# Spreading a second layer norm over the last pairs of a local attention and the first feed-forward

## What is computed

```
x = x + local_attention(ln_c(x))          # norm over channels, 7x7 windows, relative bias
t = to_tokens(x)
h = ln_t(t)                               # the second norm: (t - mean) / sqrt(var + 1e-5), over 64 channels
for step in 33 steps:
    op = argmax(h[0, 0, :19])             # the op decides which weights, and whether
    if attn_mask[step, op]: h = softmax(q k^T / 8) v wo      # an attention
    if ffn_mask[step, op]:  h = relu(h w1 + b1) w2 + b2      # and / or a feed-forward is run
out = t + h
```

## Time and profile before

| what | us |
|---|---|
| median of 3 runs | 248.5 (248.47 to 250.22) |
| the profiled execution, its own time | 249.26 |
| its span in the profile | 247.0 |
| PE busy in the span | 230.8 (93%) |
| DVE busy | 161.4 (65%) |
| ACT busy | 151.1 (61%) |

### The profile page before, as it was taken

One profiled execution on the slowest core, in us unless ns is written; L12 is line 12 of the kernel. 1 busy time (PEld: TensorE's weight loads), 2 busy tenths in 40 slices (PEclk: granted clock), 3 DMA queues, 4 the chain that ended last, 5 costly groups with the idle time before them and its releaser, 6 DMA issues.

```text
span 247.0 us, 5393 instructions
## 1 busy us (share of the span) xinstructions
PE 230.8 (93%) x1999; PEld 155.2 (63%) x2000; DVE 161.4 (65%) x300; ACT 151.1 (61%) x291; POOL 25.5 (10%) x37
## 2 busy tenths in 40 slices
PE   7679989999999998999899999999999999998991
PEld 3236658766777755533375787788888888886330
DVE  1535645676776644764596999897778778762642
ACT  2174462446456685464459988879887876682641
POOL 9600032212122100160000000000000000000000
PEclk9889999999999999999999999999999999999998
DMA  6500000000000001000100000000000000000006
GB/s 157 126 1 3 3 0 3 5 0 0 3 0 3 0 0 36 1 0 13 33 0 0 3 0 4 1 3 0 3 0 3 0 3 0 3 0 4 0 22 149
DMA packets 3151, 3.60 MB, mean 15 GB/s; under 512 B 1077, under 2 KB 2229, under 8 KB 3126
## 3 DMA queue, kind: packets, MB, share of 16 engines
q1 hardware_dynamic: 2486, 2.59, 4.4%
q10 hardware_dynamic: 544, 0.66, 1.0%
q0 software_dynamic: 96, 0.00, 0.0%
HBM read 2.21 MB, written 1.05 MB: 13 GB/s over the span
## 4 chain that ended last, share of the span: by engine, by line
PE 77%; DVE 6%; ACT 6%; issue 4%; DMA 2%; ACTq 2%; DVEq 1%
PE ps L649 12%; PE ps L635 11%; PE ps L614 11%; PE ps L702 6%; PE ps L716 6%; PE ps L478 5%; PE ps L466 4%; PE ps L441 4%; PE ps L332 3%; PE ps L445 3%; DMA rel_tab<-in_bias_tables 2%; PE ps L401 2%; DVE sq L1012 2%; ACT prob L813 2%; PE ps L455 1%
## 5 line engine op out<-in xcount | busy, mean ns | idle before, releaser
L935 ACT COPY arena<-ps 128x1024 f32<-128x1024 f32 x32 | 32.3, 1010 | 15.8 <-PE ps L635 15.6
L1155 DVE TENSOR_REDUCE negmax<-ps 128x1 f32<-128x1024 f32 x32 | 38.4, 1218 | 1.3 <-PE ps L614 1.1
L614 PE MATMUL ps<-h_st,g_st 128*128 128x512 f32 x128 | 38.6, 423 | 0.7 <-ACT late L883 0.4
L883 ACT ACTIVATE late<-ps,negmax 128x1024 f32<-128x1024 f32 x32 | 35.8, 1119 | 5.1 <-DVE negmax L1155 4.5
L635 PE MATMUL ps<-eye,late 128*128 128x128 f32 x256 | 33.5, 274 | 0.6 <-DVE late L1165 0.2
L635 PEld LDWEIGHTS ps<-eye,late 128*128 128x128 f32 x256 | 29.1, 141 | 6.9 <-DVE late L1165 2.7
L813 ACT ACTIVATE prob<-ps,negmax 128x308 f32<-128x308 f32 x32 | 16.3, 513 | 27.7 <-DVE negmax L1056 27.7
L649 PE MATMUL ps<-arena,late 128*64 128x128 f32 x512 | 31.5, 276 | 1.1 <-ACT arena L935 1.1
L649 PEld LDWEIGHTS ps<-arena,late 128*64 128x64 f32 x512 | 27.6, 137 | 3.8 <-issue 2.2
L614 PEld LDWEIGHTS ps<-h_st,g_st 128*128 128x128 f32 x128 | 21.7, 188 | 8.8 <-issue 3.2
L1165 DVE TENSOR_SCALAR late<-late,rinv 128x1024 f32<-128x1024 f32 x32 | 24.1, 754 | 1.1
(11 more groups left out here) (120 smaller groups left out, 318.9 us busy)
## 6 DMA issues: line engine op xcount, KB each, us to landing
out<-osum SPq DMA_DIRECT2D x8, 128.0 KB, 2.3
x<-in_x SPq DMA_DIRECT2D x2, 256.0 KB, 5.0
x<-in_x ACTq DMA_DIRECT2D x2, 256.0 KB, 6.0
onehot<-in_key_onehot SPq DMA_DIRECT2D x2, 133.0 KB, 2.8
w1d<-in_ffn_w SPq DMA_DIRECT2D x4, 64.0 KB, 2.4
w2p<-in_ffn_pack SPq DMA_DIRECT2D x2, 65.5 KB, 2.6
spread_w<-in_spread_mat SPq DMA_DIRECT2D x4, 32.0 KB, 5.5
mean_w<-in_mean_mat SPq DMA_DIRECT2D x1, 96.0 KB, 2.3
```

What stands on the lines that cost most here:

```text
L614: mm = nc.tensor.matmul(ps[:, 2 * h + c, :], g_st[:, b2, h, q0:q0 + P], h_st[:, b2, h, part, c * 512:c * 512 + 512], start=(part == 0), st ...
L883: nc.scalar.activation(pr[:, n % 2, :], ps[:, 2 * (n % 2):2 * (n % 2) + 2, :], ACT.Exp, bias=negmax[:, 0, n % 2:n % 2 + 1], accum_out=rows ...
L935: nc.scalar.copy(prt[:, n // 8 % 2, n % 2, :, q0:q0 + P], ps[:, bank:bank + 2, :].rearrange("p b (c q) -> p (b c) q", c=4)).then_inc(S["s_ ...
L1155: nc.vector.tensor_reduce(negmax[:, 0, n % 2:n % 2 + 1], ps[:, 2 * (n % 2):2 * (n % 2) + 2, :], mybir.AxisListType.XY, ALU.max, negate=Tru ...
```

## The change

The norm's chunks 0, 1 and 2 are taken into the pairs: pairs 8, 10 and 12 have `centre` (bank 7) ahead of the scores, and `mix` of that pair waits until ACT has squared and copied it; pairs 9, 11 and 13 have `variance` (bank 7), which ACT copies out with epsilon added (`copy_variance`), and `mix` waits for that copy. DVE takes the reciprocal of each in pairs 10, 12 and 14 (`turn_variance`), and one ACT instruction takes the root of all three (`root_three`) behind pair 14. `spread` and `scale` of chunks 0 to 2 stand around `mix(15)`. Chunk 3 goes into the first feed-forward if that stands alone (`first=True`), else ahead of the loop (`finish_norm`). The decision moves into pair 7, and `load_next` into pairs 9 (ACT, DVE) and 10 (PE). `keep_busy` in the norm is gone. In the first feed-forward the next `load_next` of ACT and DVE stands ahead of the last store.

```diff
 # PE, pairs 1 to 13
-                if p < 7:
-                    pe.wait_ge(S["mixed"], p)
+                pe.wait_ge(S["mixed"], p)
+                if p == 7:
+                    turn_row(7, x2f)
+                if p in (8, 10, 12):
+                    centre(p // 2 - 4, 7)
+                if p in (9, 11, 13):
+                    variance(1, (p - 9) // 2)
...
+                if p == 7:
+                    pe.wait_ge(S["decided"], 1)
+                if p == 10:
+                    load_next()
+                if p in (8, 10, 12):
+                    pe.wait_ge(S["centre_copied"], p // 2 + 1)
+                if p in (9, 11, 13):
+                    pe.wait_ge(S["var_copied"], (p - 7) // 2)
                 mix(p)
...
             turn_probs(14)
-            turn_row(1, x2f)
             turn_values(15)
-            centre(0)
             mix(14)
             turn_probs(15)
...
+            spread(1, 0)
+            spread(1, 1)
+            mix(15)
             spread(1, 2)
...
+                if first:
+                    pe.wait_ge(S["h_ready"], 2)
                 up(0, 0)
+                if first:
+                    centre_last()
                 up(0, 1)
+                if first:
+                    pe.wait_ge(S["h_ready"], 3)
+                    variance(1, 3)
+                    up(1, 0)
+                    down(0, (0,))
+                    spread(1, 3)
+                    down(0, (1,))
                 pe.wait_ge(S["h_ready"], chunks + 4)
-                up(1, 0)
+                if not first:
+                    up(1, 0)
                 up(1, 1)
-                down(0)
+                if not first:
+                    down(0)
 # ACT
+            def copy_variance(j):
+                act.wait_ge(S["var_ready"], 4 + j + 1)
+                nc.scalar.activation(sq[:, j * 512:j * 512 + P], ps[:, 7, 0:P], ACT.Identity,
+                                     bias=eps_c[:, 1:2]).then_inc(S["var_copied"], 1)
+            def root_three():
+                act.wait_ge(S["var_turned"], 3)
+                inv = sq[:, 0:3 * 512].rearrange("p (j c) -> p j c", j=3)[:, :, 0:P]
+                nc.scalar.activation(inv, inv, ACT.Sqrt).then_inc(S["rooted"], 1)
...
+                if p in (8, 10, 12):
+                    square(1, p // 2 - 4)
+                if p in (9, 11, 13):
+                    copy_variance((p - 9) // 2)
+                if p == 9:
+                    load_next()
                 exps(p + 2)
             copy_turned(14)
             load_table(ACT.Sqrt)
+            root_three()
             copy_turned(15)
...
                 for t in range(4):
                     relu(t, 0)
+                    if first and t == 0:
+                        square(1, 3)
                     relu(t, 1)
+                    if first and t == 0:
+                        root(1, 3)
                     if t > 0:
                         store(t - 1)
+                    if first and t == 1:
+                        load_table(ACT.Exp)
+                if first:
+                    load_next(1)
                 store(3)
 # DVE, pairs 1 to 13
                 copy_values(p + 1)
...
+                if p == 7:
+                    decide(0, 7)
                 maxima(p + 2)
                 add_mixed(p)
+                if p == 9:
+                    load_next()
+                if p in (10, 12):
+                    turn_variance(p // 2 - 5)
```

More of the change, by code:

```diff
@@ L215, in run_event, with run @@
                 load_next()
-            def run(attention, feed_forward):
+            def run(attention, feed_forward, finish_norm=None, first=None, loads_itself=False):
                 eng.reg_alu(alone, am, 1, op=ALU.logical_shift_left)
@@ L482, in mix @@
                 mm.then_inc(S["pv_done"], 1)
+            load_next, run, sections = routing(pe)
             pe.wait_ge(S["k_loaded"], 32)
@@ L691, in attention, with feed_forward @@
                 mix(15)
-            def feed_forward(a, f, ev, row):
+            def feed_forward(a, f, ev, row, first=False):
                 chunks = pe.snap(4 * pe.snap(a + f))
@@ L706, in up, with down @@
                     mm.then_inc(S["hid_ready"], 1)
[L708 to L712, removed]
+                def down(t, parts=(0, 1)):
+                    set0, bank = 4 * (t % 2), t // 2
+                    for i in parts:
+                        c = i ^ bank
                         pe.wait_ge(S["relu_act"], 8 * f + 2 * t + i + 1)
@@ L737, in feed_forward @@
                 down(3)
-            run(attention, feed_forward)
+            run(attention, feed_forward, finish_norm, partial(feed_forward, first=True))
         @block.scalar
@@ L826, in copy_turned @@
                 ins.then_inc(S["pt_copied"], 1)
+            load_next, run, sections = routing(act)
             copy_queries(0)
@@ L961, in feed_forward @@
                     relu(t, 0)
+                    if first and t == 0:
+                        square(1, 3)
                     relu(t, 1)
+                    if first and t == 0:
+                        root(1, 3)
                     if t > 0:
                         store(t - 1)
+                    if first and t == 1:
+                        load_table(ACT.Exp)
+                if first:
+                    load_next(1)
                 store(3)
-            run(attention, feed_forward)
+            run(attention, feed_forward, finish_norm, partial(feed_forward, first=True), True)
         @block.vector
@@ L1084, in add_mixed, with decide @@
                                         ALU.add).then_inc(S["mixed"], 1)
+            def decide(n, bank, ev=None):
+                dve.wait_ge(S["row_turned"], n + 1)
+                if ev is not None:
+                    dve.wait_ge(S["info_read"], readers * ev + readers)
+                dve.sem_inc(S["passed"], 1)
+                row = ps[0:1, bank, 0:NOPS]
+                nc.vector.max(top8[:], row).then_inc(S["op_max"], 1)
+                dve.wait_ge(S["op_max"], n + 1)
+                dve.sem_inc(S["passed"], 1)
+                nc.vector.max_index(idx8[:], top8[:], row).then_inc(S["decided"], 1)
+            load_next, run, sections = routing(dve)
             maxima(0)
@@ L1247, in feed_forward @@
                     relu(t, 1)
+                    if first and t == 0:
+                        inverse(1, 3)
+                        scale(1, 3, "h_ready")
                     if t == 2:
```

135 lines of the change are left out of this document (63 added, 72 removed).

## The result

| what | before | after |
|---|---|---|
| median of 4 runs each, us | 248.67 (248.47 to 250.22) | 253.02 (251.01 to 255.66) |
| ratio, with its 95% interval | | 1.0122 [1.0080, 1.0164] |
| the profiled execution, its own time, us | 249.26 | 253.53 |
| its span, us | 247.0 | 251.3 |

The changed kernel is slower by 1.2% by this ratio, which leaves out its slow run of 255.66 us (mean clock 0.969), while the median has it in; without it the median is 252.51. The forecast was 252.1, in a range of 249.4 to 253.8.

The account below looks back on a forecast made before the run. PE, busy 93%, bounds the pairs; a chain over all engines, then POOL up to store(0), bounds what follows. Pairs +4.9, behind them -2.9, attention start +0.2, clock +1.4: +3.6 on 248.5 gives 252.1 us, range 249.4 to 253.8.

Parts of the forecast that it names:

- Pair 7, +1.1: In pair 7, mix(7) waits for the decision's argmax and comes 1.12 us later; bounds 0.1 and 1.3.
- Pairs 8, 10 and 12, +0.9 each: One more 512-column product on PE lengthens each of these pairs by 0.9 us, 2.7 in all; ACT just fits.
- Pairs 9, 11 and 13, +0.36 each: A variance product on PE adds 0.36 us to each, 1.1 in all; its copy fits into ACT's idle time.
- load_next and reciprocals, 0: load_next in pairs 9 and 10 and reciprocals in 10, 12 and 14 cost no time.
- Behind the pairs, -2.9: From turn_probs(14) to the end of the fourth scale: 14.4 us instead of 17.30; bounds 2.3 and 3.5 saved.
- The table load, 1.28 and nothing more: On ACT a table load costs 1.28 us, without the page's extra drain of 1.38 per switch of sets.
- The rival with 2.8 us more: Table switches cost their drain: root(3) and qk_bd each 1.4 us later, +6.4, 254.9 us; chance 0.03.
- POOL decides store(0), +2.0 by pairs and tail: First feed-forward: POOL's additions behind the last scale release store(0), which moves by 4.9 - 2.9 = +2.0 us.
- PE's gap of 4.1 and the clock's +1.4: PE idles 4.1 us ahead of up(2, 0); the lower clock behind it costs 1.4 us, bounds 0 and 1.7.
- the clock stays up: Rival: PE's gap ahead of up(2, 0) does not lower the clock; +2.2, 250.7 us; chance 0.27.
- Start of the attention, +0.2: Between store(3) and qk_bd, load_next moves ahead and a table load comes in: 0.2 us later.
- the rival of a quicker POOL: First feed-forward: POOL's additions run faster with DVE quiet, up(2, 0) follows PE; 246.6 or 245.6 us; chance 0.12.

Follow-up runs that it names:

- e5_decide: Changed kernel with only pair 7's decision earlier (row turned right behind the probabilities, argmax ahead of normalise(8)): 253.0 us, 1.0187.
- e4_sqrt: Changed kernel with the square root's table loaded early, at the entry of the first feed-forward: 253.02 us, 1.0111.
- e9_fill_sqrt: Changed kernel with filler products on PE ahead of up(2, 0) and the square root's table loaded early: 250.36 us, 1.0069.
- e2_pool: Changed kernel with each of POOL's four additions waiting only for its own chunk of the norm: 248.11 us, 0.9976.
- e1_fill: Changed kernel with six filler products on PE in the gap ahead of up(2, 0): 251.53 us, 1.0102.
- e8_nobusy: Kernel before without its three keep_busy(0, 2) fillers in the norm: 249.78 us, 1.0029.
- e7_pool_sqrt: Changed kernel with POOL adding chunk by chunk and the square root's table loaded early: 247.94 us, 0.9918.

## Why the prediction was right, point by point

- **Pair 7, +1.1:** 4.35 against 3.22, +1.13. mix(7) is released by the argmax. e5_decide shows that this is an order on two queues and no need: without it 0.88 is saved.
- **Pairs 8, 10 and 12, +0.9 each:** 4.08 against 3.23, +0.85. ACT's two instructions hold up no mix. **Pairs 9, 11 and 13, +0.36 each:** 3.57, 3.58 and 3.57, +0.35. **load_next and reciprocals, 0:** pair 10, with PE's load_next, is as long as pair 8, and pair 9, with those of ACT and DVE, as pair 11. The pairs in all: +4.70, forecast 4.9.
- **Behind the pairs, -2.9:** -2.48. The end is at 14.82 and not at 14.4. The first steps stood where I had put them (root of three at 3.42, forecast 3.5; up(0, 0) at 6.59, forecast 6.7; centre(3) at 7.65, forecast 7.6). Mis-sized are the PE steps behind: I gave up(0, 0), the centring product and up(0, 1) 0.9 us each, and each takes 1.06 (100.25 - 99.19). So variance comes at 9.77 instead of 9.4 and the root at 11.88 instead of 11.6. The last 0.1 lies between the root and the scale.
- **The table load, 1.28 and nothing more:** the root starts at 103.42, where the load at 102.13 ends (102.13 + 1.28 = 103.41). The rival with 2.8 us more falls. The Trainium skill (ScalarE: Activation LUTs, "What ACT_TABLE_LOAD costs") gives 1.28 us for the load and 1.38 more for a drain at every switch of sets; neither ahead of this load (the relu ends at 101.42 + 0.69 = 102.11) nor behind it is there such a time. What the load cost on the chain was 1.14 us (e4_sqrt, e9_fill_sqrt). The trace has eight loads, as forecast, where the kernel before has four.
- **POOL decides store(0), +2.0 by pairs and tail:** store(0) is 2.5 later, of which 0.3 is the start. e2_pool settles it: take POOL away, and 3.25 us go.
- **PE's gap of 4.1 and the clock's +1.4:** 3.73 and 1.53. PE was done 2.1 us behind the scale and not 1.8. e1_fill shows cause and size, 1.5. The rival "the clock stays up" falls for the executions profiled; the run of 251.01 us at 0.988 may have paid less.
- **Start of the attention, +0.2:** +0.23.
- **Sum:** forecast +3.6, measured 253.02 - 248.67 = +4.35 by the medians, +3.84 by the 252.51 without the run of 255.66, and 4.26 in the spans. The mis-sizings above add 0.4 (tail) + 0.1 (clock) - 0.2 (pairs) and so cancel in part. What is left is no step of mine: the pairs began 0.3 later in this profile, and the runs scatter by more than that with their clock.
- **A slip in the chances:** "slower by over 1%" was given 0.58. The parts named for it, nearly all of 0.48, a third of 0.27, and 0.10 and 0.03, make about 0.7.

## What to carry to other kernels

Ask of every wait that counts "all of it" whether it can count one part: here that wait was free while another engine took equally long, and cost nearly 5 us, the clock's share counted in, once that engine had been relieved. When a change takes work off the busiest engine just ahead of a wait, work out what the wait is then bound by, and add what the clock takes back behind the new gap. A saving that is sure in the trace and missing in the time is to be tried again with the gap closed before it is given up.

## What the runs showed of the hardware

- **How much the clock takes differs from execution to execution.** The same gap of 3.73 us cost 1.53 us in the profile of the changed kernel, where the clock fell 1.6 us behind the end of the gap, and 12.48 - 9.57 = 2.91 in that of e4_sqrt, where it was down from the first product on. A shorter chain ahead of a gap can thus gain nothing in one execution. Whether the shorter chain itself moved the fall, or this execution happened to meet it so, is not shown: the changed kernel's own runs go from 251.01 us at 0.988 to 255.66 at 0.969.
- **Short gaps can bring it down too.** In e8_nobusy the clock fell behind an idle time of 1.44 us, with others of 0.22 and 0.33 in the ten microseconds ahead. Single gaps of 0.94 (mix(7)) and 0.5 (e2_pool) did not bring it down, nor did one of 1.13 at 17 us in the changed kernel. The Trainium skill (TensorE: Matmul & The Clock Gate, "A second HAM failure mode: psum-queue depth-cycling") tells of a clock that swings between its two levels because PE idles briefly and often between groups; e8_nobusy agrees in that short idle times were enough, but its clock fell once there and did not swing.
- **One kernel has several times.** Runs of the kernel before took 246.6 us at a mean clock of 0.997 and 0.998, 248.2 to 249.3 at 0.989 to 0.993, 249.3 to 250.3 at 0.984 to 0.986, and 251.4 and 251.7 at 0.976. In the profiles the start differs, in the stretch from 8 to 16 us, behind the wait for the first tables. In the kernel before it is 0.62, 0.50, 0.50 and 0.68 in four windows of it; in the changed kernel 0.50 from 8 to 14. From 12 to 14 and from 14 to 16 it is 0.81 and 1.00 in e2_pool, which reaches mix(6) at 62.39, and 0.50 and 0.54 in e7_pool_sqrt, which reaches it at 64.25. Where the runs at 0.976 and at 0.998 differ was not profiled. Differences of under 1 us want runs of like clock beside each other.
- **POOL's additions have one speed.** 4.94 / 4 = 1.24 us each for 128x512 f32 in the changed kernel, 3.73 / 3 = 1.24 in e2_pool, 1.27 for one alone. In the changed kernel DVE has nothing to do from 108.4 to 112.18, and the additions are no faster for it, which was the way in which the rival of a quicker POOL could have come true.
